# Centring on ACT instead of Pool in the ternary feed-forward of a four-layer decoder, one Trainium2 core

## The reference, cut to what matters

```python
def _layernorm(x, axis=-1, eps=1e-05):
    m = jnp.mean(x, axis=axis, keepdims=True)
    v = jnp.var(x, axis=axis, keepdims=True)
    return (x - m) / jnp.sqrt(v + eps)

def rmsnorm(x, weight, eps=EPS):
    var = jnp.mean(x * x, axis=-1, keepdims=True)
    return x * jax.lax.rsqrt(var + eps) * weight

def activation_quant(x):
    scale = 127.0 / jnp.clip(jnp.max(jnp.abs(x), axis=-1, keepdims=True), 1e-05, None)
    return jnp.clip(jnp.round(x * scale), -128, 127) / scale

def bitlinear(x, w):
    xq = activation_quant(x)
    wq = weight_quant(w)
    return jnp.einsum('bsh,oh->bso', xq, wq)
...
x_norm = rmsnorm(x, norm_weight)
gate_up = bitlinear(x_norm, w_gate_up)
gate, up = jnp.split(gate_up, 2, axis=-1)
hidden = jnp.square(jax.nn.relu(gate)) * up
return bitlinear(hidden, w_down)
...
x = x + jnp.tanh(g_ffn[1]) * _L1_ffn_ref(_layernorm(x, axis=-1), L1_ffn_w_gate_up, L1_ffn_w_down, L1_ffn_norm_weight)
```

## Time and profile before

| | us |
|---|---|
| median of 3 runs (lowest, highest) | 3711.77 (3710.74, 3715.72) |
| the profiled execution, its own time | 3704.24 |
| span in its profile | 3702.5 |
| PE busy in the span | 2874.9 |
| DVE busy | 2234.3 |
| ACT busy | 1493.3 |
| POOL busy | 1066.7 |

### The profile page before, as it was taken

How to read it: one execution, slowest core, us unless ns; L and a number is a source line. 1 busy time by engine, 2 the same in 40 slices (tenths; PEclk the granted TensorE clock), 3 DMA queues, 4 the chain that set the end, 5 groups by cost and what they waited for, 6 DMA issues and landing times. The chain is left out here.

```text
span 3702.5 us, 59792 instructions
## 1 busy us (share of the span) xinstructions
PE 2874.9 (78%) x19922; PEld 1817.1 (49%) x19922; DVE 2234.3 (60%) x5017; ACT 1493.3 (40%) x3096; POOL 1066.7 (29%) x1424
## 2 busy tenths in 40 slices
PE   5388884476699994559947698999979749999993
PEld 4233333332355553423323476444557638888782
DVE  7689993687577775734468697888869720000003
ACT  5267772155122224559935454222245311111110
POOL 3111110277133335412279432000033351111110
PEclk7599996699899997579968899999989759999996
DMA  8766643299422223388500242000044221111204
GB/s 267 173 115 120 119 107 137 95 372 361 146 81 80 80 79 135 126 132 123 102 1 1 104 158 64 1 1 1 1 129 139 94 71 58 47 54 50 85 28 136
DMA packets 261320, 386.33 MB, mean 104 GB/s; under 512 B 56321, under 2 KB 188654, under 8 KB 260768
## 3 DMA queue, kind: packets, MB, share of 16 engines
q1 hardware_dynamic: 234192, 312.76, 31.4%
q0 software_dynamic: 25152, 68.22, 5.3%
q10 hardware_dynamic: 1680, 1.57, 0.2%
HBM read 227.75 MB, written 160.24 MB: 105 GB/s over the span
## 5 line engine op out<-in xcount | busy, mean ns | idle before, releaser
L3120 POOL DMA_INDIRECT rows_out<-e_out,e_tr_dest x224 | 234.6, 1047 | 874.9 <-DVE e_out L3750 511.8
L1195 ACT ACTIVATE a_pt<-a_psS 128x512 f32<-128x512 f32 x512 | 277.6, 595 | 156.2 <-PE a_psS L1093 151.9
L3750 DVE COPY e_out<-e_psD 128x512 f32<-128x512 f32 x40 | 27.7, 692 | 494.0 <-PE e_psD L3718 493.9
L1217 DVE TENSOR_REDUCE a_mx_sb<-a_psM 128x4 f32<-128x1024 f32 x256 | 292.9, 1213 | 18.9 <-PE a_psM L1076 17.7
L3518 PE MATMUL e_psG<-e_wgu,e_yT 128*128 x576 | 274.9, 600 | 26.9 <-ACT e_yT L3546 24.3
L1107 PE MATMUL a_psV<-a_pt,a_vt 128*18 128x256 f32 x4096 | 293.6, 389 | 1.3 <-issue 0.8
L3718 PE MATMUL e_psD<-e_w,e_hT 128*128 128x256 f32 x1280 | 291.5, 387 | 0.0
L3707 PE MATMUL e_psH<-e_yT,e_w 128*128 128x256 f32 x1280 | 285.2, 381 | 1.6 <-issue 0.8
L3650 ACT ACTIVATE e_hT<-e_psH 128x512 f32<-128x512 f32 x160 | 95.5, 597 | 454.6 <-PE e_psH L3707 454.6
L3718 PEld LDWEIGHTS e_psD<-e_w,e_hT 128*128 128x128 f32 x1280 | 246.9, 195 | 33.7
L3707 PEld LDWEIGHTS e_psH<-e_yT,e_w 128*128 128x128 f32 x1280 | 244.7, 191 | 35.7 <-issue 2.1
(11 more groups left out here) (427 smaller groups left out, 6137.7 us busy)
## 6 DMA issues: line engine op xcount, KB each, us to landing
kbd<-e_bgu SPq DMA_DIRECT2D x64, 512.0 KB, 4.5
cr_kbd<-kbd SPq DMA_DIRECT2D x64, 512.0 KB, 3.4
rows_in<-zeros POOLq DMA_DIRECT2D x36, 522.0 KB, 6.2
e_xin<-rows_in SPq DMA_DIRECT2D x144, 128.0 KB
vbd<-e_bd SPq DMA_DIRECT2D x64, 272.0 KB, 4.6
cr_vbd<-vbd SPq DMA_DIRECT2D x64, 272.0 KB, 2.7
cq_rows<-rows_out SPq DMA_DIRECT2D x32, 512.0 KB, 5.8
e_w<-in_L_ffn_w_dram SPq DMA_DIRECT2D x16, 1024.0 KB, 7.6
```

The source lines that it names most:

```text
L1195: act.activation(pt[:, probs(t, h), b, :, :], psS[:, unit(t, h, b) % S_BANKS, :].rearrange("p (k c) -> p k c", k=KC), ACT.Exp, scale=scale ...
L1217: dve.tensor_reduce(mx[:, t % 2, :, h, :], psM[:, k % 2, :, :].rearrange("p b (f c) -> p b f c", f=2), AX_X, ALU.max).then_inc(ring_read, 1)
L3120: pool.indirect_dma_start(out=self.rows_out[0:limit, :], out_offset=bass.IndirectOffsetOnAxis(ap=self.dest[:, t:t + 1], axis=0), in_=rows, ...
```

## The change

The row constants get a second one, `shift` = -(rr * mean), made by two more operations at the end of each root chain. The centring becomes an ACTIVATE with the function Identity, scale `rr` and bias `shift`, so z = rr * x + shift. ACT's loop begins at s = -10 as Pool's does, and the centring stands at the head of each of its steps. Pool keeps the multiplication by `norm_weight`.

```diff
@@ class BitPrelude
+        self.shift = core.sb(ctx, "bp_shift", [P, TILES], F32)
...
-        c = Chain(pool, self.rooting, g, 7)
+        c = Chain(pool, self.rooting, g, 9)
...
         c.link(pool.tensor_tensor(self.rr[:, rows], self.tmp[:, 3, :], self.tmp[:, 1, :], ALU.mult))
+        c.link(pool.tensor_tensor(self.shift[:, rows], self.rr[:, rows], self.core.mv[:, rows, 0], ALU.mult))
+        c.link(pool.tensor_scalar(self.shift[:, rows], self.shift[:, rows], -1.0, None, ALU.mult))
         c.close()
@@ phase_bit, gpsimd
-                def centre(g, j):
+                def weigh(g, j):
                     t = g * G + j
-                    if g >= 2:
-                        pool.wait_ge(rounded, g - 1)
-                    pool.tensor_scalar(z[:, g % 2, j, :], core.xs[:, t, :], core.mv[:, t, 0:1], col(prelude.rr, t), ALU.subtract, ALU.mult).then_inc(centred, 1)
                     pool.wait_ge(centred, t + 1)
                     pool.tensor_tensor(z[:, g % 2, j, :], z[:, g % 2, j, :], prelude.wb[:, :], ALU.mult).then_inc(z_ready, 1)
...
-                        centre(g, j)
+                        weigh(g, j)
@@ phase_bit, scalar
-                for s in range(-2, TILES + 1):
+                def centre(g, j):
+                    t = g * G + j
+                    if g >= 2:
+                        act.wait_ge(rounded, g - 1)
+                    act.activation(z[:, g % 2, j, :], core.xs[:, t, :], ACT.Identity, bias=col(prelude.shift, t), scale=col(prelude.rr, t)).then_inc(centred, 1)
+
+                for s in range(FIRST, TILES + 1):
+                    g, j = group_at(s, 10)
+                    if g is not None:
+                        centre(g, j)
                     if s == -2:
                         for i in range(3):
                             copy_weights(i)
```

## The result

| | before | after |
|---|---|---|
| median of the comparison, us | 3715.64 (3707.02 to 3725.96, 19 runs) | 3708.41 (3697.36 to 3714.69, 19 runs) |
| the profiled execution, its own time | 3704.24 | 3697.36 |
| span in its profile | 3702.5 | 3695.6 |

The ratio is 0.9979 (95% interval 0.9971 to 0.9988): 7.8 us less by the ratio, 4.5 to 10.8 us. The forecast was a gain of 13.6 us and 3698.2 us, with a range up to 3706.5. The sign was right; the gain is a little over half, and the time lies 1.9 us above the range.

A forecast was written before the change was run, and what follows sets the result against it. The prediction took Pool to set the pace of layer 1's feed-forward, DVE next. Period 9.8 plus start 5.0 less last roots 1.2 gave 13.6 us, so 3711.8 - 13.6 = 3698.2 us, with an 8-in-10 range of 3692.5 to 3706.5.

The forecast's parts named there:

- the change of the bound: Layer 1's feed-forward, main stretch: Pool sets the pace at 5.00 us a tile; without centring the period is DVE's.
- the start: Start of layer 1's feed-forward: tile 0's product with u comes 5.0 us earlier, ends 0.6 and 6.5.
- the last two roots: Last two root chains ahead of the feed-forward: two more operations each, costing 1.2 us.
- the term of the period: Feed-forward tiles 0 to 22: 4.55 us a tile instead of 5.00, a gain of 9.8 us, ends 16.6 and 4.3.
- the attention loop that was to be shifted as a whole: Attention ahead of the feed-forward: two more operations in six of the eight roots cost nothing.
- the base to which the sum was added: Whole kernel: the 13.6 us gain was taken off 3711.8 us, the median of three runs.
- the allowance of 0.10: Feed-forward period: 4.55 us a tile taken instead of 4.45, as Pool's remaining weighting sometimes stands in DVE's way.
- The new wait: Feed-forward start: ninth centring on ACT, ahead of weight copies, waits until group 0 is rounded; gives back 2.7 us.
- the wait of DVE behind a root: Attention: DVE's reciprocal may start 0.5 us later, but DVE then idles 3.10 us for PE, so no cost.
- The centring on ACT: ACT in the feed-forward: about 0.5 us per centring, fitting ahead of the relu where ACT waits for PE; free.
- Rival 1: Feed-forward: DVE and Pool exclude each other, so the present period stays; 3708.0 us, chance 0.11.
- Rivals 2, 3 and 4: Start gives nothing, 3702.6, chance 0.10; DVE never idle, 3691.4, 0.06; slower, centring delays ACT's square, 3724.0, 0.05.

The follow-up runs named there:

- e4_no_weighting: The changed kernel with Pool's multiplication by the norm weight left out; 3692.07 us, 4.36 us a tile.
- e2_copies_first: The changed kernel with the first three batches of weight copies ahead of ACT's ninth centring; 3693.34 us, ratio 0.9965, and again 3695.69, 0.9963.
- e12_act_extra: The kernel before with 32 unused ACTIVATEs on ACT at the places of the new centrings, Pool still centring; 3702.41 and 3712.97 us in two runs.
- e7_inner_doubled: The kernel before with four more operations in each of the six inner root chains, none in the last two; 3710.74 us, ratio 1.0011.
- e16_after_fourth: The changed kernel unaltered, profiled a fourth time; 3704.80 us against 3711.38 before, ratio 0.9981.
- e5_before_again: The kernel before, unchanged, against itself, for a second profile; ratio 1.0006 (0.9996 to 1.0017).
- e6_shifts_late: e2_copies_first with all 32 shifts made by two operations behind the last root, none in the inner chains; 3697.30 us, ratio 0.9969.
- e9_centre_last: e2_copies_first with the centring behind relu and square in ACT's step instead of ahead of them; 3708.41 us, ratio 0.9978.
- e1_change_again: The changed kernel unaltered, measured and profiled a second time; 3698.96 us against 3707.91 before, ratio 0.9979.
- the three runs: Runs of the kernel before made ahead of the prediction; median 3711.77 us.
- e10_centre_twice: e2_copies_first with each centring from tile 12 on done a second time on ACT, into an unread tile; 3699.66 us.

## Why the prediction was right, and where wrong

The sign, the change of the bound, the start and the last two roots came out. Three steps failed, and each is worked out below: the term of the period (9.8 us forecast, 7.5 measured), the attention loop that was to be shifted as a whole (2.1 us longer, cause open), and the base to which the sum was added (3.9 us too low).

- **The bound.** Right: Pool set the pace and no longer does. Pool is busy 74% of the stretch, DVE 92%.
- **The period: the term that was mis-sized.** The term of 9.8 us measured 7.5. Of the missing 2.3, 1.8 are after's: the forecast's 4.55 us a tile was 4.63 (101.9 us for 22 tiles, four profiles). The other 0.5 are before's: its period is 4.97 in five profiles, not the 5.00 of the one that was read. The mechanism was right, since DVE sets the period and the weighting on Pool gets in its way; the allowance of 0.10 for that was too small, as e4_no_weighting measures 0.27. It was set on the 4.45 of steps 22 to 25, and there a second error went the other way: without the weighting the stretch takes 4.36. DVE's busy time rose, from 91.8 to 94.1 us in the mean of five and four profiles (93.3 to 94.3 in the first pair), and behind tile 0's wait its idle time is 8.4 us in after's first profile, where the row at steps 22 to 25 gave 1.2 in 17.8. Those four steps also took 18.8 us in two of the four repeats of before, and 17.7 and 17.8 in the others, so one row of them was a thin base.
- **The start.** The term of 5.0 us is 5.0; the gate product came 1.6 us earlier where 1.5 stood. The new wait that was priced at 2.7 measured 2.3 twice over, taken away (e2_copies_first) and put in alone (e12_act_extra). DVE had group 0 rounded 3.9 us earlier after the stage's start where 4.2 stood, so two small misses cancel in the 1.6. Behind tile 22 the stage gained another 0.5 us (13.0 - 5.0 - 7.5).
- **The last two roots.** 1.2 us forecast, 1.2 measured.
- **The attention loop: "the rest of the span is shifted as a whole" failed too, and its cause stays open.** In ten profiles with the two operations inside the loop it takes 248.4 us in the mean (246.1 to 250.5), in seven without, all of them with Pool's centring, 246.3 (245.7 to 247.3): 2.1 us more. What the prediction ruled on, the wait of DVE behind a root, came out as it said. In after DVE's reciprocal is released by Pool's add:

```profile
1702.52 1.76 DVE L1230 RECIPROCAL a_rec<-a_psN 128x256 f32<-128x256 f32 x1 [1.94 <-POOL xs L990]
```

  It is 0.6 us late and DVE has the 3.10 us of the earlier trace rows to make it up. Only where DVE also sums weights does an interval between two copies of PE's sums grow, the 27th by 0.4 us, and the 28th gives it back. So two operations per root cost the loop nothing by these rows (four do: the same two intervals keep 0.6 us in e7_inner_doubled). The 2.1 us lie elsewhere: 1.0 in the 4th interval and 1.0 in the 22nd and 23rd. The longer ones are mostly those in which PE stands on "issue", in the middle of a row of matmuls, while the loads keep the DMA busy (in before its share is 0.72 to 0.96 in stretches of 20 us from 1640 to 1816 us, then 0.02, and behind that no profile has such a place). Three such rows of e16_after_fourth, whose loop took 250.5 us:

```profile
1652.05 0.28 PE L1093 MATMUL a_psS<-a_qa,a_ka 48*128 48x256 bf16 x1 [2.45 <-issue]
...
1732.28 0.43 PE L1121 MATMUL a_psN<-a_ov_sb,a_pick 128*64 128x256 f32 x1 [0.76 <-issue]
...
1810.39 0.82 PE L1107 MATMUL a_psV<-a_pt,a_vt 128*18 128x256 f32 x9 [1.30 <-issue]
```

  Before has such places too, as e5_before_again shows one of 0.88 us at 1724.46. The 4th interval comes ahead of the first root and is 11.4 us in the mean of the ten and 10.4 of the seven: half of the 2.1 us arises before an added operation has run. That, the 247.4 of e7_inner_doubled (more operations, a shorter loop) and the 248.4 of e6_shifts_late (none in these chains, a longer one) speak against the time of the operations. What is left is the written program's layout, chance, or the set of runs: the three of the set of e9_centre_last have 246.1 to 247.1, no longer than before, and the four of the set of e1_change_again 247.3 to 250.5, with no profile of before beside them; in the two sets with profiles of both, the kernels with the old chains have 245.7 to 247.3 and those with the new ones 249.4 and 250.5. No run tells these apart.
- **The sum.** 13.0 - 1.2 - 2.1 = 9.7 us, a ratio of 0.9974, which lies in all four intervals; the mean of the four is 8.4 us. Of the 5.2 us between that and the forecast's 13.6, the period is 2.3, the attention loop 2.1, less 0.5 gained behind tile 22; 1.3 is within the uncertainty.
- **The time.** The third step that failed is the base: before was at 3715.64 in that comparison and not at 3711.77, and the sum took one set's median for another's. By the ratio the changed kernel would have been at 3704.0 beside the three runs. The range was missed by 1.9 us, less than each of the three, the period (2.3), the loop (2.1) and the base (3.9), so any one of them put right would have brought the time into it.
- **The centring on ACT.** 0.50 forecast, 0.592 measured, free all the same; e10_centre_twice shows room for twice as much. The row taken had one pointer operand, this instruction has two. The Trainium skill, page "ScalarE: Activation LUTs", section "What ACT_TABLE_LOAD costs", says that each pointer operand adds about 93 ns, and by that the estimate would have been 0.588. The trace agrees: 0.592.
- **Rival 1 (ports exclusive)** named 3708.0, nearly the measured time, and is wrong nevertheless: its period was to stay, and it fell by 0.34 us. Part of it is true. DVE's scaling takes 708 to 734 ns in the mean of the stretch, over four profiles, where it took 480 to 589 over five. In after, for instance, it runs beside three Pool operations:

```profile
1950.75 0.73 POOL L1971 TENSOR_TENSOR bt_z<-bt_z,bp_wb 128x256 f32<-128x256 f32 x1
1951.46 0.89 POOL L1991 TENSOR_SCALAR bt_h<-bt_h,bt_scale 128x704 f32<-128x704 f32 x1
1952.42 1.97 POOL L1995 TENSOR_SCALAR bt_q<-bt_h 128x704 bf16<-128x704 f32 x1
```

```profile
1950.86 2.75 DVE L2179 TENSOR_SCALAR bt_za<-bt_z,bt_s 128x256 f32<-128x256 f32 x4
```

  Four scalings of 0.34 us at their shortest take 2.75 us, but end at 1953.61, inside the rounding that runs from 1952.42 to 1954.39 at its usual length. One by one they take 0.77, 0.94, 0.93 and 0.34 us: the first ends 0.15 us behind Pool's weighting and the second 0.15 us behind Pool's scale, but the other two end inside the rounding. The rule of the Trainium skill, page "SBUF — State Buffer", section "SBUF: two separate sides", is that whichever of the two engines starts first gets the shared ports for its whole instruction and the other fully blocks. It fits the wait of DVE here in kind and not for the rounding.
- **Rivals 2, 3 and 4** are out: the start gave its 5.0 us, DVE did idle, and it never waited for the square behind tile 0.

## What to carry to other kernels

When an engine's load is lifted, take the new period from a stretch in which the next engine runs beside what will be left on the first; a stretch without it gives too little (here 4.45 us a tile, where 4.63 came). An instruction moved to another engine's stream brings its wait along: put it behind whatever is ready there and does not need it, which alone was worth 2.3 us of the start, but ahead of the place where its consumer wants it. Price a change against a median of the same set of runs: one kernel moved by 8 us between sets here, as much as the change is worth. And read a row that the sum rests on in several profiles: before's main stretch took 108.9 to 110.0 us in five of them.

## What the runs showed of the hardware that was not expected

- A stage far from the change took 118, 123.5 or 126 us, alike in all profiles of a set of runs (126 was seen in versions of the changed kernel alone), by idle time of ACT and PE put to "issue" or to a transfer that they don't need. What they wait for there is not shown by the profile.
- PE stands 0.4 to 2.7 us inside a row of matmuls that wait for nothing that the profile shows, at the same few tiles of the attention (the first of them, 1.35 to 2.73 us, in all 19 profiles), while the loads run (in before at a DMA share of 0.72 to 0.96).
- An ACTIVATE of 128x256 with two pointer operands takes 582 to 600 ns, one with one pointer 495.
